# Returning expert results by GpSimd scatters and plain loads instead of plain stores and gathers, with the expert copies on ScalarE

## The chip, the cores and the metric

One core of a Trainium2 chip runs the whole program. The metric is the time of one execution on the device in microseconds; less is better. TensorE (PE), VectorE (DVE), ScalarE (ACT) and GpSimd (POOL) compute, each from its own queue, and wait for each other by semaphores. SyncE (SP) only issues DMAs. GpSimd issues DMAs too, the indirect ones, in the order of its queue.

## What is computed

The program is one layer in four parts: attention over 16 sequences of 512 tokens, an expert network on the result, a state space model (mamba), and the expert network again, on the first 2048 tokens. The expert network is, for each token and each of its two experts e with weight w:

```python
h = gelu(xr @ w1A[e].T @ w1B[e], approximate=False)   # rank 64, 1024 wide
ye = h @ w2A[e].T @ w2B[e]
y = zeros((T, hs)).at[tok].add(w * ye)                # T = 2048 tokens, hs = 256, 8 experts
```

In the kernel its input is normalised first and the result is added to the token's row.

## The kernel before

The four parts follow one another with a barrier of all engines between them. `expert_ffn` (L436) is called twice, tag `f1_` and `f2_`; below they are the first and the second network. The 4096 pairs of a token and an expert are sorted by expert and padded to whole tiles of 256 rows: MT = 23 tiles, each of one expert, two halves of 128 rows (HS = 2), 46 halves in all (NH).

**Routing** is computed in the first network only (L568 to L693): `slots` (the token of each row of each tile), `places` (the row at which each pair's result stands) and `owner` (the expert of each tile). SyncE stores the three (L575 to L577), a barrier follows, and mamba and the second network load them again.

**A tile j** goes through this chain. GpSimd gathers its rows of x by two indirect DMAs (`fetch`, L748; four buffers `xg`, so tile j + 4 is fetched when tile j has been normalised). VectorE measures mean and variance (`measure`, L811 to L817), GpSimd raises to the power -0.5 (`power`, L757), VectorE normalises (L825). TensorE transposes (L942), VectorE copies (`turned`, L833), TensorE multiplies by the expert's first A matrix (`ranks`, L952), ScalarE and VectorE split the product in a high and a low part (L894, `low` L837), TensorE multiplies up in two halves (L968), ScalarE takes the Gelu (`bend`, L900), TensorE multiplies down (L981) and back to 256 columns (L992), and ScalarE copies the result to `y_sb` (`y_out`, L906). The tile's expert weights are copied from the table of all experts to tiles of their own: `s_1a` (128x256) and `s_2a` (128x512) by GpSimd (`stage`, L763 and L770), `s_hi` and `s_lo` by ScalarE and VectorE (L912, L851).

**Order.** Each engine's queue is written out by hand, skewed over tiles. In step j, GpSimd does `power(j+2)`, the two gathers of tile j + 4, `stage(j+1)`. VectorE: `turned(j+1)`, copy of c (L844), normalise j + 2, split and `low` of j + 1, `measure(j+3)`. ScalarE: bend(j, 0), split(j+1), bend(j, 1), high(j+1), y_out(j-1). TensorE: up(j, 0), transposes of j + 1, down(j-1, 1), up(j, 1), ranks(j+1), back(j-1), down(j, 0).

**Results.** SyncE stores each tile's `y_sb` to the DRAM array `y_rows` in tile order (L729). In the first network the array is read in mamba (L1318). In the second, GpSimd waits for all stores and gathers back `y_back` by 32 indirect DMAs of 128 rows (L797); in groups of four token tiles (YG = 4) VectorE weighs and adds (L884, 32 instructions), and SyncE stores the sums in 16 DMAs (L738). The token rows `x_all` (2 MB) and the weights are loaded once 11 tiles are done (L726, L727).

## Time and profile before

| what | value |
| --- | --- |
| time, median of 3 runs | 2910.95 us (2910.9 to 2911.77) |
| the profiled execution | 2913.27 us |
| its span | 2911.5 us |
| first network, from its first gather to its last y_out | 545.0 to 722.8 us |
| second network, from its first load to the end | 2663.2 to 2911.5 us |
| PE, DVE, ACT, POOL busy over the whole span | 86%, 80%, 67%, 65% |

Positions are microseconds from the span's start. A row of the trace gives start, duration, engine, line, operation, output and inputs, how many instructions it merges, and in brackets the idle time of that engine ahead of it with what ended it. A DMA row on POOL is the time in which GpSimd writes the transfer's descriptors; when the data has landed is told apart. "SPq" is SyncE issuing a DMA.

### The profile page before, as it was taken

To read this page: it belongs to the slowest core of one execution; us is meant where nothing else is said; L and a number is where in the kernel's file an instruction comes from. 1 tells how busy PE (TensorE), PEld (TensorE's weight loads), DVE (VectorE), ACT (ScalarE), POOL (GpSimd) and SP (SyncE) were. 2 spreads that over 40 slices of the span, in tenths; PEclk is the share of its full clock that TensorE was granted. 3 is DMA by queue.
4 is the path that set the end of the run, shared out by engine and by line. 5 is a ranking of instruction groups with operands and counts; after the bars stand their busy time and mean duration, and the time that the engine had idled before them with its cause. 6 is when DMAs were issued, how large, how long until landed. Compare 5 with 4: busy or idle time off the path is not lost. (4 is left out here: it accounts for less than half of the span.)

```text
span 2911.5 us, 42446 instructions
## 1 busy us (share of the span) xinstructions
PE 2515.1 (86%) x15334; PEld 1943.2 (67%) x15334; DVE 2317.3 (80%) x2353; ACT 1962.5 (67%) x2845; POOL 1880.0 (65%) x1243
## 2 busy tenths in 40 slices
PE   5999998498698999999999999999999999974892
PEld 4878786365366767767777677777777777773561
DVE  6888784465189999999999999989988889894662
ACT  3655654154588788787787887877878878760451
POOL 1212121353279889888888888887888888883454
PEclk9999999699799999999999999999999999997996
DMA  1212110522313034033141330330312302304243
GB/s 50 66 43 65 43 58 29 125 76 64 99 61 124 27 106 128 9 127 103 30 131 27 106 124 9 109 109 10 117 38 80 117 9 102 103 1 113 74 103 105
DMA packets 144739, 219.74 MB, mean 75 GB/s; under 512 B 26980, under 2 KB 111844, under 8 KB 144548
## 3 DMA queue, kind: packets, MB, share of 16 engines
q1 hardware_dynamic: 137060, 196.78, 21.4%
q0 software_dynamic: 7488, 20.46, 2.7%
q8 instruction: 115, 1.88, 0.3%
q14 instruction: 76, 0.62, 0.1%
HBM read 174.69 MB, written 42.51 MB: 75 GB/s over the span
## 5 line engine op out<-in xcount | busy, mean ns | idle before, releaser
L1381 POOL TENSOR_TENSOR m_state<-m_state,m_c_all 128x1024 f32<-128x1024 f32 x512 | 1201.2, 2366 | 212.4 <-DVE m_state L1488 211.0
L1488 DVE TENSOR_TENSOR_SCAN m_state<-m_decay,m_ps_d 128x1024 f32<-128x1024 f32 x512 | 1150.9, 2273 | 76.6 <-PE m_ps_d L1808 55.9
L1549 ACT ACTIVATE m_decay<-m_dt,m_aneg 128x511 f32<-128x511 f32 x1024 | 659.2, 709 | 33.4 <-DVE m_state L1488 32.9
L1808 PEld LDWEIGHTS m_ps_d<-m_bdiag,m_duT 128*128 128x128 f32 x4096 | 512.0, 200 | 160.8 <-issue 92.4
L1808 PE MATMUL m_ps_d<-m_bdiag,m_duT 128*128 128x128 f32 x4096 | 530.5, 285 | 74.4 <-DVE m_state L1488 73.9
L1821 PE MATMUL m_ps_y<-m_ident,m_state 128*128 128x128 f32 x4096 | 525.3, 275 | 8.1 <-POOL m_state L1381 8.0
L1821 PEld LDWEIGHTS m_ps_y<-m_ident,m_state 128*128 128x128 f32 x4096 | 471.4, 143 | 82.2 <-issue 56.3
L1476 DVE TENSOR_TENSOR m_ps_d<-m_ps_u,m_b_all 128x1024 f32<-128x1024 f32 x256 | 315.4, 1232 | 35.2 <-ACT m_ps_u L1586 19.2
L1723 PE MATMUL m_ps_f<-m_hT,m_win 128*128 128x512 f32 x512 | 262.8, 640 | 47.2 <-DVE m_dt L1443 33.0
L1746 PE MATMUL m_ps_f<-m_up,m_tap 128*128 128x512 f32 x512 | 231.7, 596 | 0.0
L188 POOL TENSOR_TENSOR a_rstd<-a_var_eps,a_neg_half 128x4 f32<-128x4 f32 x16 | 16.2, 1010 | 297.5 <-DVE a_var_eps L277 297.5
L1723 PEld LDWEIGHTS m_ps_f<-m_hT,m_win 128*128 128x128 f32 x512 | 92.6, 201 | 130.3 <-issue 69.5
L900 ACT ACTIVATE f_hid<-f_ps_up 128x1024 f32<-128x1024 f32 x92 | 94.2, 1024 | 107.8 <-PE f_ps_up L968 107.8
L1746 PEld LDWEIGHTS m_ps_f<-m_up,m_tap 128*128 128x128 f32 x512 | 92.6, 190 | 97.8 <-issue 94.6
L1610 ACT ACTIVATE m_u<-m_ps_f,m_cb 128x512 f32<-128x512 f32 x64 | 44.0, 687 | 154.5 <-PE m_ps_f L1746 154.4
L194 POOL TENSOR_TENSOR a_trig_lo<-a_trig,a_trig_hi 128x2048 fp32r<-128x2048 f32 x16 | 73.7, 4608 | 96.5 <-ACT a_trig_hi L347 96.5
L424 PE MATMUL a_ps_o<-a_vals,a_probs 128*128 128x257 f32 x512 | 118.8, 385 | 16.3 <-DVE a_xout L290 14.5
L329 ACT ACTIVATE a_probs<-a_ps_s 128x512 f32<-128x512 f32 x64 | 38.3, 599 | 138.6 <-PE a_ps_s L401 138.5
L1352 POOL TENSOR_TENSOR m_sp_l<-m_sp_l,m_sp_a 128x512 f32<-128x512 f32 x64 | 81.6, 1275 | 72.6 <-ACT m_sp_a L1569 72.3
L1792 PE MATMUL m_ps_f<-m_wout,m_z 128*128 128x256 f32 x512 | 118.4, 385 | 2.5 <-DVE m_z L1464 1.7
L424 PEld LDWEIGHTS a_ps_o<-a_vals,a_probs 128*128 128x128 f32 x512 | 94.9, 190 | 37.4 <-DVE a_xout L290 19.7
L757 POOL TENSOR_TENSOR f_rstd<-f_var_eps,f_neg_half 128x2 f32<-128x2 f32 x46 | 33.2, 723 | 129.3 <-DVE f_var_eps L817 129.3
(203 smaller groups left out, 4367.5 us busy)
## 6 DMA issues: line engine op xcount, KB each, us to landing
m_c_all<-m_bc_rows SPq DMA_DIRECT2D x128, 512.0 KB, 7.4
m_b_all<-m_bc_rows SPq DMA_DIRECT2D x64, 512.0 KB, 8.0
out<-m_xw SPq DMA_DIRECT2D x32, 512.0 KB, 3.2
f_y_rows<-f_y_sb SPq DMA_DIRECT2D x46, 256.0 KB, 2.1
a_xin<-x SPq DMA_DIRECT2D x16, 512.0 KB, 4.6
a_xres<-x SPq DMA_DIRECT2D x16, 512.0 KB, 5.3
x<-a_xout SPq DMA_DIRECT2D x16, 512.0 KB, 3.3
m_xin<-x SPq DMA_DIRECT2D x16, 512.0 KB, 5.4
```

Source lines behind the costliest of these rows:

```text
L424: ins = nc.tensor.matmul(ps_o[r][:, 0:D + 1], probs[h][:, t, s * P:(s + 1) * P], vals[h][:, t, :], start=(t == 0), stop=(t == TT - 1))
L900: nc.scalar.activation(hid[q][:, :, :], ps_up[q][:, :, :], ACT.Gelu).then_inc(gelu_done, 1)
L1352: nc.gpsimd.tensor_tensor(sp_l[:, :], sp_l[:, :], sp_a[:, :], ALU.subtract).then_inc(sp_fix, 1)
L1381: nc.gpsimd.tensor_tensor(s, s, c_all[:, n, :, :], ALU.mult).then_inc(weighed, 1)
L1476: nc.vector.tensor_tensor(ps_d[0][:, :, :], ps_u[:, :].unsqueeze(1).to_broadcast([P, 2, S]), b_all[:, n // 2, :, :], ALU.mult).then_inc(sc ...
L1488: nc.vector.tensor_tensor_scan(state[:, r, :, :].rearrange("p n t -> p (n t)"), decay[:, r, :, :].rearrange("p n t -> p (n t)"), ps_d[i % ...
L1549: ins = nc.scalar.activation(decay[:, r, j, 1:S], dt_sb[:, c % DR, 1:S], ACT.Exp, scale=aneg[:, c, n:n + 1])
L1723: ins = nc.tensor.matmul(f[:, :], win[:, k, e * P:(e + 1) * P], hT[:, k, :], start=(k == 0), stop=(k == KT - 1))
L1746: ins = nc.tensor.matmul(f[:, :], tap[:, k, s, :], up[:, k % 2, s:s + S], start=(s == 0), stop=(s == K - 1))
L1792: ins = nc.tensor.matmul(f[:, v * D:(v + 1) * D], z_sb[h][:, c, t * P:(t + 1) * P], wout[:, c, :], start=(c == 0), stop=(c == CT - 1))
L1808: ins = nc.tensor.matmul(ps_d[1][:, j, t * P:(t + 1) * P], duT[:, c % DR, t, :], bdiag[:, n // 2, TT * j + t, :], start=True, stop=True)
L1821: ins = nc.tensor.matmul(ps_y[:, t, :], state[:, i % RING, j, t * P:(t + 1) * P], id_sb[:, :], start=(n == 0 and j == 0 and t == 0), stop= ...
```

## The change

In both networks the copies of `s_1a` and `s_2a` move from GpSimd to ScalarE: `ranks_in(j+1)` behind split(j+1), ahead of bend(j, 1); `downs_in(j+1)` behind y_out(j-1). One read of `owner` serves all.

In the second network `y_rows` gets another order: 128 rows for padding, then one row for each pair, all first experts' pairs by token, then all second experts'. GpSimd scatters each half tile of `y_sb` to its pairs' rows by an indirect DMA (`scatter`), which waits until the scatter ahead of it has landed; `scatter(j-2, 0)` stands ahead of the gathers of tile j + 4 and `scatter(j-2, 1)` behind them; the last two tiles' scatters follow the loop. `y_sb` gets three buffers (YR). SyncE waits for all 46 scatters and then loads `y_back` by 8 plain DMAs of 512 rows. The routing of the first network computes the list of pair rows (`pair_row`), from which `slots` follows, and stores it as a fourth list.

```diff
+    YR = 3
...
-    y_rows = nc.dram_tensor(tag + "y_rows", [MT * TS, D], F32, kind="Internal").ap()
+    y_rows = nc.dram_tensor(tag + "y_rows", [MT * TS if first else P + TOK * TOPK, D], F32, kind="Internal").ap()
...
-                    sp.wait_ge(r_list, 3)
+                    sp.wait_ge(r_list, 4)
                     sp.dma_start(ROUTE["slots"], slots[:, :]).then_inc(r_stored, 16)
                     sp.dma_start(ROUTE["places"], places[:, :]).then_inc(r_stored, 16)
+                    sp.dma_start(ROUTE["rows"], pair_row[:, :]).then_inc(r_stored, 16)
...
-                    dve.wait_ge(r_step, 36)
-                    nc.vector.tensor_copy(slots[:, :], list_f[:, :]).then_inc(r_list, 1)
+                    dve.wait_ge(r_step, 35)
+                    nc.vector.tensor_scalar(token_f[:, :], list_f[:, :], float(P), 0.0, ALU.subtract,
+                                            ALU.max).then_inc(r_step, 1)
+                    nc.vector.tensor_scalar(later[:, :], list_f[:, :], float(P + TOK), float(TOK), ALU.is_ge,
+                                            ALU.mult).then_inc(r_step, 1)
+                    dve.wait_ge(r_step, 37)
+                    nc.vector.tensor_tensor(slots[:, :], token_f[:, :], later[:, :], ALU.subtract).then_inc(r_list, 1)
+                    nc.vector.tensor_scalar(list_lo[:, :], list_f[:, :], 0.0, column[:, 0:1], ALU.is_equal,
+                                            ALU.mult).then_inc(r_step, 1)
+                    dve.wait_ge(r_step, 38)
+                    nc.vector.tensor_tensor(pair_row[:, :], list_f[:, :], list_lo[:, :], ALU.add).then_inc(r_list, 1)
...
+            sp.wait_ge(y_ready, MT // 2)
+            sp.dma_start(g_w[:, :, :], weights.rearrange("(t p) k -> p t k", p=P)).then_inc(x_loaded, 16)
+            sp.dma_start(x_all[:, :, :], xf[0:TOK, :].rearrange("(t p) d -> p t d", p=P)).then_inc(x_loaded, 16)
+            sp.wait_ge(y_spread, 16 * NH)
+            for g in range(NT // YG):
+                for k in range(TOPK):
+                    sp.dma_start(y_back[:, k * NT + g * YG:k * NT + (g + 1) * YG, :],
+                                 y_rows[P + k * TOK + g * YG * P:P + k * TOK + (g + 1) * YG * P, :]
+                                 .rearrange("(t p) d -> p t d", p=P)).then_inc(y_got[g], 16)
...
+            def scatter(j, h):
+                n = HS * j + h
+                if h == 0:
+                    pool.wait_ge(y_ready, j + 1)
+                if n:
+                    pool.wait_ge(y_spread, 16 * n)
+                nc.gpsimd.indirect_dma_start(y_rows, bass.IndirectOffsetOnAxis(pair_row[:, n:n + 1], 0),
+                                             y_sb[j % YR][:, h, :], None).then_inc(y_spread, 16)
...
+                if j >= 2 and not first:
+                    scatter(j - 2, 0)
                 if j + XR < MT:
-                    fetch(j + XR)
-                if j + 1 < MT:
-                    stage(j + 1)
+                    for h in range(HS):
+                        fetch(j + XR, h)
+                if j >= 2 and not first:
+                    scatter(j - 2, 1)
             if first:
                 return
-            for r in range(2):
-                pool.wait_ge(y_stored[r], 16 * ((MT - r + 1) // 2))
-            for t in range(NT):
-                for k in range(TOPK):
-                    c = k * NT + t
-                    nc.gpsimd.indirect_dma_start(y_back[:, c, :], None, y_rows,
-                                                 bass.IndirectOffsetOnAxis(places[:, c:c + 1], 0))\
-                        .then_inc(y_got[t // YG], 16)
+            for j in range(MT - 2, MT):
+                for h in range(HS):
+                    scatter(j, h)
+            pool.wait_ge(y_spread, 16 * NH)
...
+                if not first and j >= YR:
+                    act.wait_ge(y_spread, 16 * HS * (j - YR + 1))
+                nc.scalar.activation(y_sb[j % (2 if first else YR)][:, :, :], ps_y[:, :, :], ACT.Copy).then_inc(y_ready, 1)
...
+            def ranks_in(j, e):
+                if j == 0:
+                    act.wait_ge(w_loaded, 16 * 2 * KT)
+                if j >= 2:
+                    act.wait_ge(a_full, j - 1)
+                nc.scalar.activation(s_1a[j % 2][:, :, :],
+                                     w_1a[:, :, bass.ds(e, 1), :, :].rearrange("p k a h r -> p k (a h r)"),
+                                     ACT.Copy).then_inc(s_ranked, 1)
+
+            def downs_in(j, e):
+                if j >= 2:
+                    act.wait_ge(down_done, 2 * j - 2)
+                if j == 0:
+                    act.wait_ge(down_loaded, 48)
+                nc.scalar.activation(s_2a[j % 2][:, :, :], w_2a[:, :, bass.ds(e * R, R)], ACT.Copy)\
+                    .then_inc(s_downed, 1)
...
+            e = expert(0)
+            ranks_in(0, e)
             act.wait_ge(up_loaded, 64)
-            split(0)
+            split(0, e)
             high(0)
             for j in range(MT + 1):
+                if j == 0:
+                    downs_in(0, e)
                 if j < MT:
                     bend(j, 0)
                 if j + 1 < MT:
-                    split(j + 1)
+                    e = expert(j + 1)
+                    split(j + 1, e)
+                    ranks_in(j + 1, e)
                 if j < MT:
                     bend(j, 1)
                 if j + 1 < MT:
                     high(j + 1)
                 if j:
                     y_out(j - 1)
+                if j + 1 < MT:
+                    downs_in(j + 1, e)
```

Two places in the queues. GpSimd in the second network, one step (`rstd` is `power`, `xg` a gather, `s_1a` and `s_2a` the copies; L768, L777 and L785 are the new lines of gather, power and scatter). Before:

```order
L757 TENSOR_TENSOR f2_rstd1<-f2_var_eps1,f2_neg_half 128x2
L748 DMA f2_xg3<-out,f2_slots 128x256 x2
L760 TENSOR_LOAD f2_owner
L760 ISA x2
L763 ISA
L763 COPY f2_s_1a0<-f2_w_1a 128x256
L770 ISA
L770 COPY f2_s_2a0<-f2_w_2a 128x512
```

and of the change:

```order
L777 TENSOR_TENSOR f2_rstd1<-f2_var_eps1,f2_neg_half 128x2
L785 DMA f2_y_rows<-f2_y_sb1,f2_pair_row 4224x256
L768 DMA f2_xg3<-out,f2_slots 128x256 x2
L785 DMA f2_y_rows<-f2_y_sb1,f2_pair_row 4224x256
L777 TENSOR_TENSOR f2_rstd0<-f2_var_eps0,f2_neg_half 128x2
```

Both copies and the read of `owner` are gone from the step, and a scatter stands on either side of the two gathers.

ScalarE in the second network, from one bend(j, 0) (`hid0`) to the next. Before:

```order
L900 ACTIVATE f2_hid0<-f2_ps_up0 128x1024
L909 TENSOR_LOAD f2_owner
L909 ISA x2
L912 ISA
L912 ACTIVATE f2_s_hi0<-f2_w_1b 128x512
L900 ACTIVATE f2_hid1<-f2_ps_up1 128x1024
L894 ACTIVATE f2_a_split0<-f2_ps_a 128x256
L906 ACTIVATE f2_y_sb0<-f2_ps_y 128x512
L900 ACTIVATE f2_hid0<-f2_ps_up0 128x1024
```

and of the change:

```order
L929 ACTIVATE f2_s_hi0<-f2_w_1b 128x512
L937 ISA
L937 ACTIVATE f2_s_1a0<-f2_w_1a 128x256
L916 ACTIVATE f2_hid1<-f2_ps_up1 128x1024
L910 ACTIVATE f2_a_split0<-f2_ps_a 128x256
L924 ACTIVATE f2_y_sb2<-f2_ps_y 128x512
L946 ISA
L946 ACTIVATE f2_s_2a0<-f2_w_2a 128x512
L916 ACTIVATE f2_hid0<-f2_ps_up0 128x1024
```

The copy of `s_1a` now stands between `s_hi` and the second bend, that of `s_2a` behind the copy of the results.

## Rows read from the trace of the kernel before

**Rows 1.** The page: the chain that ended last, by line

```profile
POOL f_y_back L797 1%; POOL f_xg L748 1%; DMA f_w_2b<-w2b 1%; PE f_ps_c L981 0%; POOL f_s_2a L770 0%; POOL f_s_1a L763 0%; PE f_ps_up L968 0%; SPq L530 0%; POOLq L760 0%; PE f_ps_y L992 0%; SPq L526 0%; PE f_ps_a L952 0%; POOL f_rstd L757 0%; DVE f_x_all L884 0%; SPq L521 0%
```

**Rows 2.** Timeline, second network, one step: start, duration, instruction, idle before

```profile
2757.50 1.03 POOL L748 DMA_INDIRECT f_xg<-out,f_slots  x1 [0.20 <-issue]
...
2759.21 1.70 DVE L825 TENSOR_SCALAR f_xn<-f_xg,f_mv,f_rstd 128x256 f32<-128x256 f32 x2
...
2759.78 0.41 POOL L763 COPY f_s_1a<-f_w_1a 128x256 f32 x1
...
2760.25 1.13 PE L952 MATMUL f_ps_a<-f_xT,f_s_1a 128*128 128x256 f32 x4 [0.53 <-POOL f_s_1a L763]
...
2761.42 0.38 ACT L894 ACTIVATE f_a_split<-f_ps_a 128x256 fp32r<-128x256 f32 x1 [0.63 <-PE f_ps_a L952]
2761.84 0.42 DVE L837 TENSOR_TENSOR f_a_split<-f_ps_a,f_a_split 128x256 fp32r<-128x256 f32 x1 [0.33 <-ACT f_a_split L894]
2762.18 0.74 DVE L811 BATCH_NORM_STATS2 f_stats<-f_xg 128x6 f32<-128x256 f32 x2
...
2763.53 0.72 POOL L757 TENSOR_TENSOR f_rstd<-f_var_eps,f_neg_half 128x2 f32<-128x2 f32 x1 [2.78 <-DVE f_var_eps L817]
```

**Rows 3.** Stages: length, busy PE PEld DVE ACT POOL, clock, DMA, GB/s

```profile
2718.51:2725.47 6.96, 6.42 (x52) 4.29 (x52) 4.84 (x12) 3.64 (x6) 3.66 (x6) 1.00 0.25 77
...
698.97:705.33 6.36, 6.36 (x55) 4.39 (x53) 4.10 (x12) 3.54 (x5) 1.67 (x3) 1.00 0.14 45
```

**Rows 4.** Timeline of PE, first network: ranks of tiles 1 and 19

```profile
566.89 1.30 PE L952 MATMUL f_ps_a<-f_xT,f_s_1a 128*128 128x256 f32 x3
...
692.62 1.13 PE L952 MATMUL f_ps_a<-f_xT,f_s_1a 128*128 128x256 f32 x4 [0.44 <-POOL f_s_1a L763]
```

**Rows 5.** Timeline of ACT, second network, a step in which GpSimd gathers no more

```profile
2847.76 0.62 ACT L912 ACTIVATE f_s_hi<-f_w_1b 128x512 fp32r x1
...
2849.35 1.02 ACT L900 ACTIVATE f_hid<-f_ps_up 128x1024 f32<-128x1024 f32 x1 [0.97 <-PE f_ps_up L968]
...
2853.19 1.02 ACT L900 ACTIVATE f_hid<-f_ps_up 128x1024 f32<-128x1024 f32 x1 [1.33 <-PE f_ps_up L968]
```

**Rows 6.** Timeline, first network, last of the routing's three stores

```profile
543.45 0.34 SPq L577 DMA_DIRECT2D r_owner<-f_owner  x1
```

**Rows 7.** Timeline, second network's start

```profile
2699.28 0.61 POOL L770 COPY f_s_2a<-f_w_2a 128x512 f32 x1 [10.51 <-DMA f_w_2b<-w2b]
...
2703.65 2.08 PE L952 MATMUL f_ps_a<-f_xT,f_s_1a 128*128 128x256 f32 x4 [5.59 <-POOL f_s_1a L763]
```

**Rows 8.** DMA issues: queue, count, KB each, median us from issue to landing

```profile
f_y_rows<-f_y_sb SPq DMA_DIRECT2D x46, 256.0 KB, 2.1
...
f_y_back<-f_y_rows,f_places POOLq DMA_INDIRECT x32, 2.8
```

**Rows 9.** Gathers (L748) issued from 2783 to 2790, while x_all is loaded

```profile
DMA to landing us min/median/max: 6.4/6.6/6.8
```

**Rows 10.** Gathers (L748) issued from 2797 to 2804

```profile
DMA to landing us min/median/max: 3.9/3.9/4.0
```

**Rows 11.** Timeline, second network's end

```profile
2859.78 0.60 ACT L906 ACTIVATE f_y_sb<-f_ps_y 128x512 f32<-128x512 f32 x1 [3.02 <-PE f_ps_y L992]
2862.80 1.03 POOL L797 DMA_INDIRECT f_y_back<-f_y_rows,f_places  x1 [13.62 <-DMA f_y_rows<-f_y_sb]
...
2902.22 0.95 POOL L797 DMA_INDIRECT f_y_back<-f_y_rows,f_places  x1 [0.30 <-issue]
2904.93 3.75 DVE L884 SCALAR_TENSOR_TENSOR f_x_all<-f_y_back,f_g_w,f_x_all 128x256 f32<-128x256 f32 x8 [6.33 <-DMA f_y_back<-f_y_rows,f_places]
```

**Rows 12.** Stages in the same columns: weight loads, then the load of x_all

```profile
2672.00:2676.00 4.00, 0.00 (x0) 0.00 (x0) 0.00 (x0) 0.00 (x0) 0.00 (x0) 0.50 1.13 194
...
2788.00:2792.00 4.00, 3.92 (x29) 2.70 (x30) 2.84 (x8) 1.59 (x3) 1.22 (x3) 1.00 1.05 348
```

**Rows 13.** Timeline of DVE, first network: normalising with no gather in the way

```profile
572.35 0.73 DVE L825 TENSOR_SCALAR f_xn<-f_xg,f_mv,f_rstd 128x256 f32<-128x256 f32 x2
```

More of the change, by code:

```diff
@@ L464, in expert_ffn @@
         ROUTE["places"] = nc.dram_tensor("r_places", [P, NC], I32, kind="Internal").ap()
+        ROUTE["rows"] = nc.dram_tensor("r_rows", [P, NH], I32, kind="Internal").ap()
         ROUTE["owner"] = nc.dram_tensor("r_owner", [1, MT], I32, kind="Internal").ap()
@@ L485, in expert_ffn @@
         places = sb("places", [P, NC], I32)
+        pair_row = sb("pair_row", [P, NH], I32)
         owner = sb("owner", [1, MT], I32)
@@ L711, in expert_ffn @@
         c_sb = [sb(f"c_sb{r}", [P, TS]) for r in range(2)]
-        y_sb = [sb(f"y_sb{r}", [P, HS, D]) for r in range(2)]
+        y_sb = [sb(f"y_sb{r}", [P, HS, D]) for r in range(2 if first else YR)]
         block = ctx.enter_context(nc.Block())
@@ L718, in _ @@
                 sp.dma_start(slots[:, :], ROUTE["slots"]).then_inc(r_loaded, 16)
-                sp.dma_start(places[:, :], ROUTE["places"]).then_inc(r_loaded, 16)
+                sp.dma_start(pair_row[:, :], ROUTE["rows"]).then_inc(r_loaded, 16)
                 sp.dma_start(owner[:, :], ROUTE["owner"]).then_inc(r_loaded, 16)
@@ L723, in _ @@
                 load_weights(sp)
-            for j in range(MT):
-                if j == MT // 2 and not first:
-                    sp.dma_start(g_w[:, :, :], weights.rearrange("(t p) k -> p t k", p=P)).then_inc(x_loaded, 16)
-                    sp.dma_start(x_all[:, :, :], xf[0:TOK, :].rearrange("(t p) d -> p t d", p=P)).then_inc(x_loaded, 16)
-                sp.wait_ge(y_ready, j + 1)
-                sp.dma_start(y_rows[j * TS:(j + 1) * TS, :].rearrange("(h p) d -> p h d", p=P),
-                             y_sb[j % 2][:, :, :]).then_inc(y_stored[j % 2], 16)
-            if first:
-                sp.wait_ge(r_stored, 48)
+            if first:
+                for j in range(MT):
+                    sp.wait_ge(y_ready, j + 1)
+                    sp.dma_start(y_rows[j * TS:(j + 1) * TS, :].rearrange("(h p) d -> p h d", p=P),
+                                 y_sb[j % 2][:, :, :]).then_inc(y_stored[j % 2], 16)
+                sp.wait_ge(r_stored, 64)
                 for r in range(2):
@@ L742, in _, with fetch @@
         def _(pool):
-            def fetch(j):
-                if j >= XR:
+            def fetch(j, h):
+                if j >= XR and h == 0:
                     pool.wait_ge(xn_ready, j - XR + 1)
-                for h in range(HS):
-                    n = HS * j + h
-                    nc.gpsimd.indirect_dma_start(xg[j % XR][:, h, :], None, xf,
-                                                 bass.IndirectOffsetOnAxis(slots[:, n:n + 1], 0))\
-                        .then_inc(x_got[j % XR], 16)
+                n = HS * j + h
+                nc.gpsimd.indirect_dma_start(xg[j % XR][:, h, :], None, xf,
+                                             bass.IndirectOffsetOnAxis(slots[:, n:n + 1], 0))\
+                    .then_inc(x_got[j % XR], 16)
             def power(j):
@@ L779, in _ @@
             for j in range(2, XR):
-                fetch(j)
-            pool.wait_ge(w_loaded, 16 * 2 * KT)
-            stage(0)
+                for h in range(HS):
+                    fetch(j, h)
             for j in range(MT):
@@ L903, in y_out, with split @@
                 act.wait_ge(y_full, j + 1)
-                if j >= 2:
+                if first and j >= 2:
                     act.wait_ge(y_stored[j % 2], 16 * (j // 2))
-                nc.scalar.activation(y_sb[j % 2][:, :, :], ps_y[:, :, :], ACT.Copy).then_inc(y_ready, 1)
-            def split(j):
-                e = act.value_load(owner[0:1, j:j + 1], min_val=0, max_val=E - 1)
+                if not first and j >= YR:
+                    act.wait_ge(y_spread, 16 * HS * (j - YR + 1))
+                nc.scalar.activation(y_sb[j % (2 if first else YR)][:, :, :], ps_y[:, :, :], ACT.Copy).then_inc(y_ready, 1)
+            def split(j, e):
                 if j >= 2:
```

42 lines of the change are left out of this document (18 added, 24 removed).

## Prediction

> **What bounds the kernel now.** I began with the chain that ended last [rows 1]. Two of its links belong to this change: L797, the gathers that bring results back, and L748, the gathers of x, with L763 and L770, GpSimd's copies, behind them. All shares are small because only the second network, 248 us of 2911.5, stands ahead of the end; the first network shows the same steps and is followed by a barrier, so what it loses or gains moves everything after it.
>
> Next the timeline of one step [rows 2]. It is a ring: GpSimd's two gathers from 2757.50, at once the copy of s_1a (0.41), which TensorE's ranks waits for (0.53 idle), then high on ScalarE, low and measure on VectorE, and at 2763.53 GpSimd's power, which had waited 2.78 us for the variance; then gathers again. So nobody is full, and the ring turns in 6.96 us with TensorE busy for 6.42 of them [rows 3]. Where GpSimd has no gathers left, the same step takes 6.36 us, all of them TensorE's [rows 3]. Granted clock is 1.00 of 2.4 GHz in both.
>
> Last the end [rows 11]: y_out ends at 2860.38, the first of 32 gathers starts at 2862.80, the last at 2902.22 (31 pitches of 1.27 us), and four blocks of weighing, 3.75 us each, sit behind the groups. From y_out to the end it is 51.1 us, of which 39.4 are GpSimd writing descriptors.
>
> **The change, part by part.**
>
> *Copies to ScalarE.* This opens the ring: ranks waits for GpSimd no more. ScalarE has a gap of 0.97 us ahead of the second bend and 1.33 ahead of the first [rows 5]. s_1a has as many columns as high (0.38) [rows 2], s_2a as many as split (0.62) [rows 5], so both fit and I cost them at nothing; ranks starts 1.9 us after the transposes end and s_1a should be ready at about 1.6. With that cover gone it would be some 0.3 us a step. TensorE is late next: 6.36 a step.
>
> First network: ranks of tile 1 is at 566.89, of tile 19 at 692.62 [rows 4]; 18 steps of 6.36 give 681.4, so -11.2 us. The last tiles run at 6.36 already [rows 3]. Routing gets four more short VectorE operations ahead of the stores (0.2 each with their waits: 0.9) and one more store (0.34 and a gap) [rows 6]: +1.3. GpSimd keeps gathers and power there and has slack. Sum -9.9.
>
> Second network, start: w_2b lands at 2699.2 and GpSimd's copy waits 10.5 us for it [rows 7]; in the change ScalarE waits, with bend(0, 0) queued behind, then 0.62 + 1.02 + 0.62 + 0.40: ranks of tile 1 at 2702.1 instead of 2703.65, and that of tile 2, without its half microsecond of waiting, near 2709.3.
>
> *Scatters.* Each step gets two indirect DMAs, and takes two copies off. GpSimd's own work is 4 x 1.27 + 0.9 = 6.0 us, under 6.36. What decides is the new wait: a scatter starts only when the one ahead has landed. From scatter 0 over two gathers to scatter 1 pass 3 x 1.27 = 3.8 us, enough to hide its landing; from scatter 1 to the next step's scatter 0 only power lies between, so that pause is the whole round trip, r. The step is 3.8 + r.
>
> No row shows a scatter. Bounds of its landing: 2.1 us, a plain store, also towards DRAM, and 2.8, a gather of 128 rows by the same engine [rows 8]; upwards 3.9 to 4.0, which gathers took in some stretches of the second network [rows 10]. I take 2.8: same descriptors, same engine, same size. To that comes 0.3 us from landing to the start of the waiting row (y_rows stored at 2860.4 + 2.1, gather at 2862.80) [rows 11]. So r = 3.1, and the step 6.9: now GpSimd, not TensorE, sets the second network's pace, hardly faster than 6.96.
>
> The Trainium skill (DMA: Bandwidth & Descriptors, Anatomy of one DMA) says that most of a DMA's fixed 2 us is the receipt of the write, and that HBM is the heaviest target. By its fit a scatter would take 2.3 us, an estimate, and the step would be TensorE's; by its remark on HBM it would be longer than the gather. The rows contradict the remark as far as they go, since the store towards DRAM lands sooner than the gather into SBUF; they differ in who writes the descriptors.
>
> Now in time: the first scatter is due when power has run after measure of tile 4, 4.2 us after ranks of tile 2: 2713.5. 17 steps of 6.9 bring the scatter of tile 17 to 2830.8. The load of x_all holds up one scatter as it did gathers, 6.6 instead of 2.8 [rows 9]: +3.8, 2834.6. From there GpSimd has no gathers and the scatters run one after another at 3.1: two for tile 17, ten for tiles 18 to 22; the last lands at 2834.6 + 11 x 3.1 + 2.8 = 2871.5. TensorE is done well before (power of tile 22 near 2840, last y_out near 2860), so the backlog of scatters, not the network, ends this part.
>
> *Loads.* SyncE's 8 loads carry 4.2 MB. x_all, rows of 1 KB into 128 partitions as here, moved at 348 GB/s [rows 12]: the first group's 1 MB lands after 2.0 + 3.1 = 5.1 us, each further one after 3.1, less than the 3.75 of weighing. Weighing is then without gaps: 4 x 3.78 = 15.1 us. The last store took 2.8 us to the end (2911.5 - 2908.7). The end is 2871.5 + 5.1 + 15.1 + 2.8 = 2894.5, that is -17.0.
>
> Sum: -9.9 - 17.0 = -26.9 us. Against the profiled execution, 2913.3, that is 2886.4; its runs' median stands 2.3 lower, so I put the forecast at **2884**.
>
> **The rivals.**
>
> *Scatters land like stores (2.1).* r is 2.4, the step is TensorE's 6.36, the last scatter lands near 2853.7 and the end is 2876.8: -34.7 - 9.9, so **2866**. For it: target and size [rows 8]. Against it: GpSimd takes 1 us for descriptors ahead of any byte [rows 2].
>
> *Landing is slow in a stretch.* Gathers took 3.9 to 4.0 in several steps after x_all [rows 10], at little DMA load. At r = 4.3 both pauses count and a step is 8.6; six such steps cost 6 x 1.7 = 10: **2894**, and 2904 if the last scatters are slow too.
>
> *Slower than before: the chain of scatters.* Place: GpSimd's wait on the scatter ahead, 17 steps and 11 more in a row. Up to r = 3.8 each 0.1 us costs 28 x 0.1 = 2.8 us, beyond it 4.5, since then scatter 1 waits too. r = 3.8 gives 2904, and r = 3.96, a landing of 3.66, eats all 26.9 us. At 4.0 throughout, the time is **2926**. For it: gathers of this engine took that long in a stretch [rows 10]. Against it: the 32 gathers at the end had a median of 2.8 [rows 8]. The remark on HBM of the Trainium skill, cited above, would lead here.
>
> *Collisions of GpSimd and VectorE.* The pair of normalisings takes 1.70 us beside gathers [rows 2] and 0.73 with none in the way [rows 13]. Four indirect DMAs a step instead of two make such a meeting likelier. VectorE has room: 4.8 us of work in 6.96 [rows 3]. If instead the DMA is held up, 0.4 in each of 17 steps, it is +7: **2891**. The Trainium skill (SBUF — State Buffer, Who interferes with whom) says that GpSimd cannot write descriptors while such a VectorE operation holds the shared port, and that whoever is second waits; the row on the pair agrees that one of them waits.
>
> *Loads at the rate of the weight loads, 194 GB/s* [rows 12]: 2.0 + 21.6 + 3.75 + 2.8 = 30.2 behind the last scatter instead of 23.0, +7.
>
> *The copies come late on ScalarE*: 0.3 us in each step of the first network, +5.
>
> **How the numbers follow.** My forecast, within 8 us of 2884, gets 0.42 (the last three rivals included where they are small), scatters like stores 0.26, slow in a stretch or one of the last three in full 0.20, a landing near break-even 0.06, slow throughout 0.06. The range takes in all but the last two: 2864, a little under the fast case, to 2904. A measurement of this kernel can tell 0.2%, 5.8 us, from no change: faster needs under 2905.1, slower over 2916.8. So faster 0.88, same 0.06, slower 0.06.
>
> **What would show it.** In the profile after: steps of 6.36 in the first network with TensorE never idle ahead of ranks; in the second, steps near 6.9, with GpSimd's idle time ahead of a scatter ended by the scatter before it, and landings of 2.8; x_all's load visible as one long step; ten scatters in a row at 3.1 us after the last normalising; then loads landing every 3 us and VectorE weighing without gaps. Steps of 6.36 in the second network make the fast rival right; steps over 7 the slow ones. Weighing with gaps would show that loads, not VectorE, set the end. Steps of over 6.4 in the first network would show the copies late.

## The result and the profile after

| | before | changed |
|---|---|---|
| median of 7 runs, us | 2910.06 | 2901.24 |
| lowest, highest | 2905.88, 2911.77 | 2898.86, 2905.51 |
| profiled execution, its span | 2913.27, 2911.5 | 2905.51, 2903.7 |

The ratio is 0.9971, with an interval of 0.9961 to 0.9981: 8.8 us faster, where 26.9 were forecast. The gain is a third of what the sum said. 2901 lies in the range, near its upper end, but in part by luck: TensorE's late increments, told below, are in none of the rivals.

The chain that ended last, by engine and by line, of the changed kernel (its answer to [rows 1]):

```profile
DMA 3%; PE 2%; issue 2%; POOL 1%; DVE 1%; SPq 1%; ACT 0%; DVEq 0%; POOLq 0%; ACTq 0%
DMA f_y_rows<-f_y_sb,f_pair_row 2%; PE f_ps_c L1026 1%; DMA f_w_2b<-w2b 1%; POOL f_xg L768 1%; PE f_ps_up L1013 1%; DVE f_x_all L900 0%; POOL f_y_rows L785 0%; DMA f_y_back<-f_y_rows 0%; PE f_ps_t L987 0%; SPq L535 0%; PE f_ps_a L997 0%; DVE f_s_lo L867 0%; DVE f_xn L841 0%; SPq L531 0%; PE f_ps_y L1037 0%
```

The gathers that bring results back are gone from it. The scatters' landings (f_y_rows) stand first, with 2% of the span. Stages of the changed kernel, in the columns of [rows 3]: two steps of the first network, with gathers and without, then two of the second.

```profile
620.06:626.87 6.81, 6.42 (x54) 4.41 (x52) 3.89 (x12) 4.16 (x7) 2.69 (x4) 1.00 0.24 79
701.00:707.36 6.36, 6.36 (x55) 4.37 (x53) 2.42 (x5) 4.37 (x7) 0.00 (x0) 1.00 0.12 41
2733.66:2740.91 7.25, 6.42 (x52) 4.29 (x52) 3.90 (x12) 4.25 (x8) 4.42 (x5) 1.00 0.29 72
2815.28:2822.99 7.71, 6.43 (x55) 4.41 (x53) 4.03 (x11) 4.15 (x7) 4.48 (x6) 1.00 0.32 68
```

Two things speak against the forecast. With gathers a step of the first network takes 6.81 us, not 6.36: 0.15 better than before. In the second network the two steps shown are 7.25 and 7.71, longer than the 6.96 of before, at the same granted clock. The timeline of GpSimd there, one step (start, duration, instruction, idle before and its releaser), and its last four scatters:

```profile
2762.88 1.16 POOL L785 DMA_INDIRECT f_y_rows<-f_y_sb,f_pair_row  x1 [1.47 <-DMA f_y_rows<-f_y_sb,f_pair_row]
2764.34 0.98 POOL L768 DMA_INDIRECT f_xg<-out,f_slots  x1 [0.30 <-issue]
2765.63 0.95 POOL L768 DMA_INDIRECT f_xg<-out,f_slots  x1 [0.30 <-issue]
2766.89 1.01 POOL L785 DMA_INDIRECT f_y_rows<-f_y_sb,f_pair_row  x1 [0.30 <-issue]
2767.93 0.73 POOL L777 TENSOR_TENSOR f_rstd<-f_var_eps,f_neg_half 128x2 f32<-128x2 f32 x1
2770.13 1.04 POOL L785 DMA_INDIRECT f_y_rows<-f_y_sb,f_pair_row  x1 [1.47 <-DMA f_y_rows<-f_y_sb,f_pair_row]
...
2868.79 0.97 POOL L785 DMA_INDIRECT f_y_rows<-f_y_sb,f_pair_row  x1 [2.18 <-DMA f_y_rows<-f_y_sb,f_pair_row]
2871.47 0.97 POOL L785 DMA_INDIRECT f_y_rows<-f_y_sb,f_pair_row  x1 [1.72 <-DMA f_y_rows<-f_y_sb,f_pair_row]
2874.63 0.97 POOL L785 DMA_INDIRECT f_y_rows<-f_y_sb,f_pair_row  x1 [2.19 <-DMA f_y_rows<-f_y_sb,f_pair_row]
2877.31 0.97 POOL L785 DMA_INDIRECT f_y_rows<-f_y_sb,f_pair_row  x1 [1.71 <-DMA f_y_rows<-f_y_sb,f_pair_row]
```

This is the chain as forecast, and a little longer: scatter 0 to scatter 1 of a tile 4.01 us here, scatter 1 to the next tile's scatter 0 3.24. Among the last four the pitch alternates: 2.68 to a second half tile, 3.16 to a first one. SyncE's loads and VectorE's weighing at the end, which answer to [rows 11]:

```profile
2879.73 8.58 SPq L754 DMA_DIRECT2D f_y_back<-f_y_rows  x8
2885.12 3.76 DVE L900 SCALAR_TENSOR_TENSOR f_x_all<-f_y_back,f_g_w,f_x_all 128x256 f32<-128x256 f32 x8 [22.45 <-DMA f_y_back<-f_y_rows]
2889.85 11.09 DVE L900 SCALAR_TENSOR_TENSOR f_x_all<-f_y_back,f_g_w,f_x_all 128x256 f32<-128x256 f32 x24 [0.97 <-DMA f_y_back<-f_y_rows]
```

From the first load to the end it is 24.0 us, forecast 23.0.

### The profile page after: what moved, and what is told of

It reads as the page before. It is cut to its first block and busy times, and to the rows that moved or that the text cites. A ratio compares the mean times of both kernels' runs of the same rounds, so it can differ in the third digit from the quotient of the medians.

```text
span 2903.7 us, 42331 instructions
## 1 busy us (share of the span) xinstructions
PE 2515.0 (87%) x15334; PEld 1944.6 (67%) x15334; DVE 2285.2 (79%) x2356; ACT 1994.6 (69%) x2937; POOL 1852.0 (64%) x1165
## 5 line engine op out<-in xcount | busy, mean ns | idle before, releaser
L1013 PE MATMUL f_ps_up<-f_a_split,f_s_hi 64*128 64x256 f32 x736 | 82.7, 313 | 29.4 <-DVE f_a_split L853 12.0
```

What stands on the lines that cost most here:

```text
L1013: ins = nc.tensor.matmul(ps_up[q][:, 2 * half + f, :], part[j % 2][side, cols], a_split[j % 2][side, x_part, :], start=(n == 0), stop=(n = ...
```

## The experiments

Eighteen more runs, some of them of the same kernel again, were made in five sessions, each on one chip and beside runs of the kernel before; the comparison above is session A, those below are B to F. Each expectation stands ahead of its result; where several stand together, the results follow in their order.

**What the copies bring, what the scatters bring (session B).** The copies alone (copies_only) are the kernel before with ScalarE's part of the change; the scatters alone (scatter_only) are the changed kernel with ScalarE as before and GpSimd's `stage` back:

```diff
 copies_only, against the kernel before (GpSimd's side; stage itself and ScalarE's side left out)
                 if j + XR < MT:
                     fetch(j + XR)
-                if j + 1 < MT:
-                    stage(j + 1)
 scatter_only, against the changed kernel (the same left out)
                     for h in range(HS):
                         fetch(j + XR, h)
+                if j + 1 < MT:
+                    stage(j + 1)
                 if j >= 2 and not first:
                     scatter(j - 2, 1)
```

> The kernel before with only the two copies of A weights moved to ScalarE, in both networks (results stored by tile, fetched back by 64 indirect loads, as before). Theory 1 (the first network's gain is only that of a step of 6.78 us against 6.96, and the second network would run the same 6.78 while it gathers): about 4 us less in each network, so 2901 to 2903 us, and then the scatter as a whole has brought nothing. Theory 2 (the scatter's side of the change brought part of the 8.8 us): this kernel stays at 2904 to 2907. In both, the windows of the first network read 6.78 a step; if they read 6.36, the change to the routing or the gathers' issue by halves was at fault.

Measured: 2886.55 us, ratio 0.9916 (0.9903 to 0.9928), better than either theory and than the changed kernel in A. (It fetches results back by the 32 indirect DMAs of before; the 64 of the note is a slip.) Windows of a step of each network:

```profile
616.23:622.57 6.34, 6.34 (x54) 4.36 (x53) 3.86 (x12) 4.37 (x7) 2.67 (x4) 1.00 0.26 82
2736.23:2742.59 6.36, 6.36 (x55) 4.37 (x53) 3.87 (x12) 4.37 (x7) 2.70 (x4) 1.00 0.26 82
```

Here the 6.36 is there, in both networks, with TensorE busy for all of it.

> The changed kernel with the two copies back on GpSimd in both networks, between the gathers and the second scatter. Theory 1 (GpSimd's queue is then the bound of the second network): two scatters, two gathers, the power and two copies in one queue give 4.0 us of issues, about 2.9 of copies and 3.2 from the second scatter to the next first one, 10.1 us a step against 7.24, over some 18 steps +52 us, and the first network back at 6.96, +4: about 2957 us. Rival: the copies hide in the wait for the scatter's landing, the step stays near 7.3, and the time is about 2905 us.

Measured: 2926.15 us, ratio 1.0051 (1.0039 to 1.0064), slower than before, between the two. Its steps in the second network are mostly 8.7 to 9.3 us (10.1 forecast): the copies do hide part of the landing. So at this point the copies were worth 22 us and the scatters as built less than nothing, and the first network's 6.8 was not the copies' doing. That left two questions, the first network and the chain.

**The first network's 0.45 us.** In the changed kernel's trace (timelines of PE, GpSimd and ScalarE, one step) the second bend begins 1.45 us behind its matmuls:

```profile
626.65 0.29 PE L1013 MATMUL f_ps_up<-f_a_split,f_s_lo 64*128 64x256 f32 x2
626.87 1.13 PE L997 MATMUL f_ps_a<-f_xT,f_s_1a 128*128 128x256 f32 x4
625.53 1.02 POOL L768 DMA_INDIRECT f_xg<-x,f_slots  x1 [0.19 <-issue]
626.86 0.95 POOL L768 DMA_INDIRECT f_xg<-x,f_slots  x1 [0.31 <-issue]
625.92 0.40 ACT L937 ACTIVATE f_s_1a<-f_w_1a 128x256 f32 x1
628.39 1.02 ACT L916 ACTIVATE f_hid<-f_ps_up 128x1024 f32<-128x1024 f32 x1 [2.07 <-PE f_ps_up L1013]
```

TensorE has gone on to ranks and s_1a is done; the bend waits for `up_done`, 0.58 us beyond the end of GpSimd's second gather.

```diff
             e = expert(0)
             ranks_in(0, e)
+            ranks_in(1, expert(1))
+            e = expert(0)
...
                     split(j + 1, e)
-                    ranks_in(j + 1, e)
...
                     downs_in(j + 1, e)
+                if j + 2 < MT:
+                    ranks_in(j + 2, expert(j + 2))
```

> The changed kernel with the copy of s_1a moved on ScalarE's queue: no longer between s_hi and the second Gelu, but behind the copy of s_2a at the end of the step, one tile earlier than before. Theory 1 (what stands in front of the second Gelu on ScalarE makes it start 1.4 us late): the second Gelu starts when its matmuls end, steps of the first network 6.36 to 6.4 instead of 6.78, -7 us there, and up to -3 in the second network's last steps: 2891 to 2894 us. Theory 2 (GpSimd's gathers hold up whatever ScalarE does next, wherever the copy stands): a Gelu or another instruction still starts 0.6 us behind the end of the second gather, steps stay 6.7 to 6.8, the time within 2 us of 2901.

Measured (copies_behind): 2893.78 us, ratio 0.9943 (0.9930 to 0.9956), and steps of 6.36, as Theory 1 had it. But the next kernel of the session, with only `YR = 4` in place of 3 (yr4), has the changed kernel's first network word for word:

> The changed kernel with four result buffers instead of three. Theory 1 (the second network's last steps of 7.9 us are a ring of scatter, y_out and the Gelu ahead of it, not a lack of buffers): y_out does not wait for y_spread, so no change, within 1 us of 2901. Theory 2 (y_out waits for the landing of the tile three back and delays what stands behind it): the last five steps fall from 7.9 to 7.24, -3.5 us, and perhaps -1 before them.

It took 2894.49 us, ratio 0.9944 (0.9931 to 0.9957), its first network runs 6.36 a step as well, and its second keeps the last steps of 7.9. So neither the place of the copy nor the fourth buffer explains it; the 7 us between these and the changed kernel of session A had another source. Beside the copies alone, in the same session, both are 7 to 8 us slower: that much the scatters cost on this chip. I looked at the trace's semaphore records for it. Times of the last matmul of up(j, 1), of the increment of `up_done`, and of the bend that waits for it:

```
                            matmul ends   increment   bend starts
changed kernel, session A      626.94       628.37       628.39
changed kernel, session C      626.73       626.74       626.77
```

The increment itself was late. The changed kernel was then run again, unchanged:

> The changed kernel once more, not one character different. In its first profile TensorE's semaphore increments came up to 1.44 us behind the last matmul while GpSimd issued one indirect transfer close behind another, so that the second Gelu started late and the steps took 6.78 us. The kernel with four buffers has the same first network, instruction by instruction, and had steps of 6.36 us and no late increment. Theory 1 (the late increments belong to the occasion on which the changed kernel was run, a chip or a placement, not to its program): first network 6.36 a step, about 2894 us like the one with four buffers. Theory 2 (something of this very program, an address or a semaphore's place, brings them): 6.78 a step again, 2901 us.

> The changed kernel a third time, unchanged. Theory 1 (the late semaphore increments of the first profile were of that occasion): first network 6.36 us a step, no increment of TensorE over 0.25 us late, 2895 to 2898 us. Theory 2 (they come and go with this program): some steps of 6.78 again, 2899 to 2902.

> The changed kernel unchanged. Theory 1 (late increments are a chip's trait): the count of TensorE increments over 0.25 us late is either none here and in all four kernels of this call, with 2894 to 2897 us, or some 85 and more in all four, with 2898 to 2902. Theory 2 (they come by the kernel or by chance): they show in some kernels of the call and not in others.

Measured (after_again, after_third, after_fourth): 2896.9 us (ratio 0.9945, 0.9932 to 0.9959) in session C, 2898.83 (0.9957, 0.9944 to 0.9971) in D and 2900.9 (0.9971, 0.9958 to 0.9983) in E. The first network's steps are 6.36 in C, as Theory 1 of the first note had it, but 6.72 in D, where the second note's Theory 1 fails, and 6.78 in E. The third note's Theory 1 holds by the table, but for the copies' 64.

The counts of TensorE's increments in the two networks (326 in each kernel) that come 0.25 to 3 us behind their matmul:

```
session A  before 0*    changed 81
session B  copies 0     scatters 0      copies_behind 0   yr4 0
session C  changed 0    scatter_free 0  early_table 0     free_early 0
session D  changed 85   own_rows 81     two_back 104      x_early 86
session E  changed 83   copies 64       two_back 105      scatter_free 115
session F  before 0     copies_spaced 0
(* its profile may be of another chip than the changed kernel's)
```

None, or 64 and more, in all kernels of a session: a trait of the session, that is of its chip or the chip's state then, and not of a kernel. (Sessions B to F had five different chips; which one A had is not known.) The same step in session C:

```profile
626.45 0.28 PE L1013 MATMUL f_ps_up<-f_a_split,f_s_lo 64*128 64x256 f32 x2
626.66 1.13 PE L997 MATMUL f_ps_a<-f_xT,f_s_1a 128*128 128x256 f32 x4
625.82 0.95 POOL L768 DMA_INDIRECT f_xg<-x,f_slots  x1 [0.30 <-issue]
626.77 1.02 ACT L916 ACTIVATE f_hid<-f_ps_up 128x1024 f32<-128x1024 f32 x1 [0.66 <-PE f_ps_up L1013]
```

Of the late increments of A, 80 of 81 were due while GpSimd was writing an indirect DMA or up to 0.5 us later, against 88 of the 239 that came on time, and none comes in the last steps of the first network, where GpSimd gathers no more. Their median is 0.86 us. For VectorE and ScalarE the records do not tell: in A one increment of ScalarE is late, but 20 of VectorE's and 27 of ScalarE's have no record at all within 3.2 us. Missing records go with the late ones. Each profile of D and E and the one of A has 16074 to 16416 records of semaphore updates, each of the others 17392 to 17420. Whether the recording itself, and not only GpSimd's descriptors, holds the increments up is a rival that no run here tests. The kernel before reads 2909 to 2911 in every session, so it isn't hurt by it; the copies alone are, by 13 us between B and E:

> The copies alone once more, beside the changed kernel on the same chip. Theory 1 (the copies bring 22 us, and the chain of waiting scatters gives 8 to 12 of them back): 2884 to 2890 us, below the changed kernel by 8 to 12. If this chip is one with late increments of TensorE's semaphores, its first network too runs 6.7 to 6.8 a step, and it reads 2890 to 2896, still below the changed kernel.

It took 2899.44 us, ratio 0.9965 (0.9952 to 0.9977), no better than the changed kernel beside it (2900.9), with the steps at 6.8 that the note foresaw, and above the range given. Why the kernel before is spared was the last question:

> The kernel before, unchanged, to have its profile in another session. Ratio 1.000 within 0.1%. Theory 1 (on a chip of the late kind its increments are late too, and its ring through GpSimd hides them): some tens of TensorE increments over 0.25 us late and steps of 6.96 all the same. Theory 2 (they are on time because its increments fall elsewhere beside GpSimd's work): none late. On a chip of the other kind both see none, and the question stays open.

```diff
 copies_spaced, against copies_only
                         .then_inc(x_got[j % XR], 16)
+                    if h == 0 and j >= XR:
+                        nc.gpsimd.tensor_tensor(idle[:, j, :], neg_half[:, :], neg_half[:, :], ALU.mult)
```

> The copies alone on ScalarE, and a product of 128x2 on GpSimd between the two gathers of a tile. Theory 1 (the increments are held while two indirect transfers are issued close behind each other): few or none late on a chip of the late kind, first network 6.36 us a step, 2885 to 2889 us on any chip. Theory 2 (any indirect transfer holds them): late as before, 6.8 us a step, 2896 to 2900 on such a chip.

Session F's chip showed no late increment in either (ratios 1.0005, 0.9995 to 1.0014, and 0.9924, 0.9907 to 0.9940; 6.36 a step), so both are without an answer.

**The chain of scatters.** In session C, without late increments, the second network can be read against the forecast, and its waits taken away. Every scatter gets padding rows of its own, so that no two write the same row (scatter_free):

```diff
-    y_rows = ... P + TOK * TOPK ...
+    y_rows = ... P + TOK * TOPK + NH * P ...
-                if n:
-                    pool.wait_ge(y_spread, 16 * n)
-                ... .then_inc(y_spread, 16)
+                ... .then_inc(y_spread[j % YR], 16)
```

> The changed kernel with padding rows of its own for every scatter (46 x 128 rows behind the pairs' rows), so that no two scatters write the same row and none waits for another; the results' buffers come free by a semaphore each. Theory 1 (the wait for the landing of one scatter before the next is the bound of the second network): GpSimd's queue holds 4.0 us of issues and 0.7 of power a step, TensorE is the bound again at 6.36, ranks(22) near 2825 as with the copies alone, the last scatter lands some 15 us later, and 24 us of loads, weighing and stores follow: 2864 to 2868 us. Rival (two scatters in flight share the queue and land one behind the other anyway, 2.9 us each, or slower): steps 6.4 to 7, and a tail with the same 3 us a scatter: 2880 to 2890 us.

Measured: 2864.89 us, ratio 0.9837 (0.9824 to 0.9851), Theory 1. GpSimd's timeline of one step, and then the window of a step:

```profile
2754.67 1.04 POOL L789 DMA_INDIRECT f_y_rows<-f_y_sb,f_pair_row  x1 [0.20 <-issue]
2756.02 0.99 POOL L774 DMA_INDIRECT f_xg<-out,f_slots  x1 [0.30 <-issue]
2757.32 0.97 POOL L774 DMA_INDIRECT f_xg<-out,f_slots  x1 [0.30 <-issue]
2758.59 1.01 POOL L789 DMA_INDIRECT f_y_rows<-f_y_sb,f_pair_row  x1 [0.30 <-issue]
2760.11 0.72 POOL L783 TENSOR_TENSOR f_rstd<-f_var_eps,f_neg_half 128x2 f32<-128x2 f32 x1 [0.52 <-DVE f_var_eps L838]
2761.04 1.04 POOL L789 DMA_INDIRECT f_y_rows<-f_y_sb,f_pair_row  x1 [0.20 <-issue]
```

```profile
2744.12:2750.47 6.35, 6.35 (x55) 4.37 (x53) 3.98 (x12) 4.37 (x7) 5.17 (x6) 1.00 0.27 85
```

GpSimd now waits for VectorE's measure, and TensorE is full. Is it the wait, or the rows? Session D took them apart, with the rows kept and the wait for the scatter before put back (own_rows_wait), and with a wait for the one two back (two_back):

```diff
 two_back, against scatter_free
+                if j:
+                    pool.wait_ge(y_spread[h], 16 * j)
                 nc.gpsimd.indirect_dma_start(y_rows, ...
-                ... .then_inc(y_spread[j % YR], 16)
+                ... .then_inc(y_spread[h], 16)
```

> Padding rows of its own for every scatter, as in the kernel that ran free, but each scatter still waits for the landing of the one before: the rows without the freedom. Theory 1 (the wait alone is what the free kernel saved): as the changed kernel, 2895 to 2898 us, steps of 7.15 to 7.9 in the second network. Rival (128 scatters' padding falling on the same 128 rows of memory made each landing slow): landings shorter than 2.9 us, steps near 6.4, 2870 to 2885.

2899.28 us, ratio 0.9960 (0.9946 to 0.9974): as the changed kernel beside it, 2898.83. The rows alone bring nothing; the wait was the cost, as Theory 1 said.

> The same rows, and each scatter waits for the landing of the one two back, the same half of the tile before. Theory 1 (one landing of 2.9 us fits beside the other work as soon as two may be in flight): a scatter two back was issued at least 4 us earlier, the wait is over before it begins, TensorE bounds the steps at 6.36, and the time is that of the free kernel, 2863 to 2868; only the tail may lose 1 us. Rival (with two in flight each lands in twice the time): 2880.

2879.29 us, ratio 0.9890 (0.9875 to 0.9905), 19.5 below the changed kernel beside it and 14 above the free kernel of session C: the rival's number. Session E ran both together:

> A wait for the scatter two back, beside the free kernel on the same chip. Theory 1 (the wait for two back is over before it begins, and the 2879 of the other session were late increments): within 1.5 us of scatter_free2. Rival (two back still holds the chain): over 5 us above it.

> No waits between scatters. On a chip without late increments 2863 to 2868 us as before; on one with them 6.75 us for some 36 steps instead of 6.36, so 2874 to 2882, as two_back read there.

2890.73 us (0.9935, 0.9919 to 0.9952) and 2892.68 (0.9945, 0.9928 to 0.9962). The wait for two back costs nothing that shows, as Theory 1 said; so the rival's number in D was not the rival's doing. But the free kernel is 28 us slower than in session C, where 9 to 17 were expected, and two_back 11 us slower than in D, with late increments in both. GpSimd's and ScalarE's timelines in scatter_free2:

```profile
2737.71 0.99 POOL L774 DMA_INDIRECT f_xg<-out,f_slots  x1 [0.31 <-issue]
2739.01 0.96 POOL L774 DMA_INDIRECT f_xg<-out,f_slots  x1 [0.30 <-issue]
2740.27 1.01 POOL L789 DMA_INDIRECT f_y_rows<-f_y_sb,f_pair_row  x1 [0.30 <-issue]
2738.41 0.41 ACT L942 ACTIVATE f_s_1a<-f_w_1a 128x256 f32 x1
2742.23 1.02 ACT L921 ACTIVATE f_hid<-f_ps_up 128x1024 f32<-128x1024 f32 x1 [3.42 <-remote]
```

The matmul that this bend waits for ended at 2738.07, and its increment came at 2742.21, 0.9 us behind the last of the three DMAs written meanwhile; TensorE's increments of 2740.00 and 2740.94 came at 2742.27 and 2742.33, right behind it. So with four indirect DMAs close together an increment is held up for 4.1 us, and steps of this kernel take up to 10.2 us. In two_back such a delay of over 3 us comes once in D and four times in E; why it is rarer in D stays open.

**Two smaller terms.** A Gelu of 128x2 was put ahead of ScalarE's wait for the A weights of the second stage, since in the changed kernel a table load of 1.28 us stands behind that wait (early_table; free_early has it beside the free scatters):

```diff
             high(0)
+            act.wait_ge(consts_set, 1)
+            nc.scalar.activation(warmed[:, :], neg_half[:, :], ACT.Gelu)
```

> The changed kernel with a Gelu of 128x2 on ScalarE before it waits for the A weights of the second stage, so that the table load of 1.28 us stands in front of that wait. Theory 1: the first tile of the second network is that much earlier and everything behind it too, -1.3 us against the same kernel without it (2894 to 2892.5, or 2901 to 2899.5 where the first network runs at 6.78). Rival (GpSimd's chain of scatters, not ScalarE, sets the second network's length, and the first scatter starts no earlier): no change.

> Both edits together: separate padding rows and the early table load. Theory 1: TensorE is the bound of the whole second network, so that the 1.3 us show in full: 2862.5 to 2867 us. Rival: as for the separate padding rows, 2880 to 2890 us, and the table load nothing.

2892.44 us (0.9929, 0.9915 to 0.9942) against 2896.9 (0.9932 to 0.9959), and 2863.87 (0.9833, 0.9820 to 0.9847) against 2864.89. The sign is the expected one both times and the intervals overlap; the 1.3 us are not shown. And x_all (2 MB; the note's 4 MB is a slip), by taking SyncE's `wait_ge(y_ready, MT // 2)` away (x_early):

> The changed kernel with the load of the residual rows and weights (4 MB and 16 KB) issued at the start of the second network, behind its weights, instead of at tile 11. Theory 1 (that load stood between two scatters and held the chain for 5.2 us more than a usual step): the step of 12.4 us becomes 7.2, and the load runs beside the first gathers, where the chain of scatters has not begun: 2 to 5 us less, 2891 to 2894. Rival (it delays the first gathers and so the whole network by as much): no change or up to 4 us more.

2899.23 us (0.9956, 0.9943 to 0.9970) against 2898.83: no gain, but intervals this wide can't tell 2 to 5 us from none. The long step is gone (7.5 instead of 11.0 in after_third), and from the first scatter to the end the profile has 3.6 us less (189.1 against 192.7). The first scatter is 2.5 us later, 2708.29 against 2705.82; 1.9 of that is there at the second network's first load already (2656.19 against 2654.33) and is none of this edit's doing. So whether the edit is worth anything stays open.

The best kernel measured has free scatters and the early table: 2863.87 us, 47 below before, on a chip of the one kind. On chips of the other kind two_back was best, 2879.29 in D, 32 below before, and 2890.73 in E, 19 below, where the free scatters read 2892.68.

## Why the prediction was wrong

The direction held, and the size failed at two steps of the sum: "TensorE is late next: 6.36 a step", and "The step is 3.8 + r" with r = 3.1. The profiled span of session A is 2903.7, that of C, without late increments, 2895.1, and the forecast one 2884.6 (2894.5 - 9.9). So of the 19.1 us missing in A, 10.5 are missing in C too, which is the chain of scatters, and 8.6 are A's alone. (A's profiled execution was its slowest; by medians A's own part is 4.3.)

**"TensorE is late next: 6.36 a step" in the first network.** On the chips of B, C and F this was right to the hundredth: the copies alone have ranks of tile 22 at 698.78 instead of 711.67, -12.9 where -11.2 was forecast without the routing, and the changed kernel in C has it at 702.94, -8.7. On A's chip it was wrong, 707.36, -4.3, since the steps with gathers are 6.78. The whole of A's excess over C is there by the second network's first scatter, 2710.97 against 2701.91, 9.1 us: 4.4 by the first network's last ranks, 2.0 more by the second network's first load, and 2.7 in its first tiles. The 2.0 are mamba's, whose stretch between the two varies from 1947.0 to 1952.5 us over the twenty profiles, whatever the kernel. None is added behind it (8.6 at the end), where the chain of scatters, not the bend, sets the pace. The mechanism I had no row for is TensorE's late semaphore increments. The rival "copies come late on ScalarE", and my sentence that steps over 6.4 would show it, named the wrong cause: s_1a ended at 626.32, ahead of the ranks at 626.87 that read it.

**"The step is 3.8 + r", r = 3.1.** In C the first scatter is at 2701.91 (forecast 2703.6, 1.7 better, since the second network's first load came 2.5 us sooner than summed; its start left out ScalarE's table load of 1.28 us). Scatter 0 of tile 17 is at 2835.99, 134.1 later where the sum had 121.1: +13.0. Of this x_all's step is +1.7 (12.4 instead of 10.7). The last four steps before tile 17, 7.9 to 8.0 each, are +4.2 against 6.9: landings of the second halves there took 3.3 us instead of 2.5, and why stays open. The other twelve make up the remaining 7.1: they begin with 8.44, the usual ones are 7.15, and 7.45 to 7.85 where scatter 1 waits too or a landing was longer. The landing wasn't the fault: it is 2.5, not 2.8. What I mis-sized is the way from landing to the next start. In GpSimd's last scatters above it is 2.7 to a second half but 3.2 to a first one: the first one waits for two semaphores, y_ready and y_spread, the second for one. After a landing of 2.4 that is 0.3 us, as I took from [rows 11], and 0.75. The order of the two waits or what else differs between the two halves was not tried. So r = 2.46 + 0.78 = 3.24, and with 3.91 instead of 3.8 for the three issues the usual step is 7.15.

The Trainium skill (DMA: Bandwidth & Descriptors, Anatomy of one DMA), whose fit gave 2.3 us for the landing, was nearer to the measured 2.5 than the gather's 2.8; its remark on HBM was not borne out, since the gathers beside, which write to SBUF, took 3.5. The rival of a landing like a store's, with a step of 6.36, failed all the same: of the 2.4 us that it had from one start to the next, the landing alone took all.

**The deeper fault: no sum for the copies alone.** I charged the second network's chain at 6.9 and compared it with the 6.96 of before, as if it cost nothing. With the copies gone GpSimd's ring was open there as well, so the true comparison was 6.36. From ranks of tile 22 to the end the copies alone need 62.8 us, the changed kernel 49.3 (C): the plain loads save 13.5. Up to ranks of tile 22 its second network needs 21.2 us more (195.0 against 173.9 from the first load). The waits cost more than the loads save; copies alone 2886.55, both 2896.9, on chips without late increments (with them the two are level, 2899.44 and 2900.9 in E). So the direction held thanks to the copies: from its first load to the end the second network takes 248.3 us before (246.3 in F), 244.3 with the whole change (C) and 236.7 with the copies alone (B). The -17.0 that the sum gave it came out as -2 to -4.

**What held.** The tail: from scatter 0 of tile 17 to SyncE's loads 36.2 us, forecast 36.9. Loads, weighing, store: 23.0 as forecast in C, where weighing has no gaps (14.75 for 32); 24.0 in A, which has one of 0.97. Routing: its last store is issued 1.46 us later, forecast 1.3. Slower than before never came, since no landing reached 3.66 over a whole network.

**A reading that was wrong.** The rival "Collisions of GpSimd and VectorE" took the 1.70 us of a pair of normalisings [rows 2] as a meeting with gathers. In the changed kernel the pair reads:

```profile
626.43 0.76 DVE L841 TENSOR_SCALAR f_xn<-f_xg,f_mv,f_rstd 128x256 f32<-128x256 f32 x2
```

It stands beside a gather too. Over both networks one normalising takes 0.41 us in the median in the changed kernel, whether it meets a DMA that GpSimd writes (46 of them) or not (46). In the kernel before, the 75 that meet GpSimd's copies of s_1a or s_2a take 0.55 to 1.08, and the 17 that don't take 0.41. So what VectorE met were the copies, and moving them away ended it; it changed no term of the sum, since VectorE had room. The Trainium skill (SBUF — State Buffer, Who interferes with whom) says of such a VectorE operation and GpSimd that whoever comes second at their shared port waits. The rows on the copies agree. Of the case that the prediction cited it for, GpSimd's writing of descriptors, these medians show nothing.

## What to carry to other kernels

When an edit bundles two changes, work out the sum for each alone: the one that opens a ring lowers the bound against which the other must be judged. A wait that guards only dummy rows can be removed by giving each writer dummy rows of its own; here that brought 32 us (2896.9 to 2864.89 in C). And where the gain is a few tenths of a microsecond a step, run it in several sessions before believing its size: here the same program was 0.9945 on one chip and 0.9971 on another.

## What the runs showed of the hardware

- On the chips of sessions D and E, and in the profile of A, TensorE's semaphore increments arrive late, by 0.6 to 0.9 us in the median of those under 3 us and up to 4.1, beside GpSimd's indirect DMAs; on those of B, C and F none of 326 does, at the same granted clock of 1.00. The copies alone lose 0.43 us a step by it (6.79 against 6.36), the free scatters up to 3.8 in some steps. The profiles with late increments also lack about 1000 of 17400 records of semaphore updates. What the chips differ in, whether the recording takes part, and why the kernel before is spared, stays open.
- An indirect DMA that waits for two semaphores started 0.5 us later behind its landing than one that waits for one (pitches 3.16 and 2.68); that the second wait is the reason was not tried by itself.
- A VectorE normalising of 128x256 took up to 1.08 us where it met GpSimd's copies, and 0.41 in the median otherwise, beside indirect DMAs that GpSimd was writing too.
- A scatter of 128 rows of 1 KB to DRAM landed 2.5 us from its start, sooner than a gather of the same size, 3.5 us in the second network and 2.8 in the first. The DMA issues of the changed kernel in C, count and median us to landing:

```profile
f_xg<-out,f_slots POOLq DMA_INDIRECT x46, 3.5
f_y_rows<-f_y_sb,f_pair_row POOLq DMA_INDIRECT x46, 2.5
```
